# Pool computes the negated score maxima of groups 2 to 31; divisions of the first batch and the mask rows change their places

## The reference

```python
# layer 0, per batch
xn  = x * rsqrt(mean(x*x) + 1e-6) * rms_w
xm  = xn * (1 + scale) + shift            # scale, shift = cond @ w_cond
q, k, v = split(xm @ w_qkv);  q, k = rope(q), rope(k)
x   = softmax(q k^T / 4) v @ w_out + x
# layer 1, per batch
xn  = layer_norm(x)
q, k, v = xn @ q_w + q_b, xn @ k_w + k_b, (xn @ v_w + v_b) * mask
y   = softmax(q k^T + (1 - mask) * -1e6) v
h   = silu(layer_norm(y) * (1 + scale1) + shift1) @ out_w + out_b
out = x + h
```

## Time and profile before

| what | us |
|---|---|
| median of three runs | 509.48 |
| the profiled execution | 507.94 |
| its span, first to last instruction | 506.1 |
| TensorE busy | 486.6 |
| VectorE busy | 397.9 |
| ScalarE busy | 343.6 |
| Pool busy | 301.4 |

### The profile page before, as it was taken

How to read it: one execution, slowest core, us unless ns; L and a number is a source line. 1 busy time by engine, 2 the same in 40 slices (tenths; PEclk the granted TensorE clock), 3 DMA queues, 4 the chain that set the end, 5 groups by cost and what they waited for, 6 DMA issues and landing times.

```text
span 506.1 us, 9691 instructions
## 1 busy us (share of the span) xinstructions
PE 486.6 (96%) x3205; PEld 177.7 (35%) x3205; DVE 397.9 (79%) x1030; ACT 343.6 (68%) x676; POOL 301.4 (60%) x387
## 2 busy tenths in 40 slices
PE   8999899999699999999999999999999999999997
PEld 3554322332153233332342233433333333332234
DVE  3867887988768679875889679986899999999224
ACT  2652467758548677676858677686778778777863
POOL 6479958999977672479507872459882045005401
PEclk9999999999989999999999999999999999999999
DMA  7764255443522443026422352015311112111011
GB/s 250 199 194 174 76 182 177 148 138 119 166 86 65 111 137 100 18 75 178 108 65 66 104 155 70 3 42 149 104 43 45 44 47 83 42 44 44 2 41 41
DMA packets 41577, 49.79 MB, mean 98 GB/s; under 512 B 12388, under 2 KB 34036, under 8 KB 41272
## 3 DMA queue, kind: packets, MB, share of 16 engines
q1 hardware_dynamic: 33336, 31.84, 21.7%
q0 software_dynamic: 7904, 16.03, 10.5%
q10 hardware_dynamic: 288, 1.31, 0.7%
HBM read 27.62 MB, written 19.01 MB: 92 GB/s over the span
## 4 chain that ended last, share of the span: by engine, by line
PE 66%; DVE 20%; DMA 4%; issue 4%; POOL 3%; ACT 2%; SPq 1%; DVEq 0%; POOLq 0%; ACTq 0%
PE bank L602 16%; PE bank L585 11%; PE bank L648 9%; DVE masked L958 9%; PE bank L576 8%; PE bank L564 8%; PE bank L676 5%; DVE row_max L961 5%; PE bank L659 5%; DMA tables<-in_tables 2%; ACT probs L787 1%; PE bank L633 1%; DMA X<-in_x 1%; PE bank L617 1%; DMA k_parts<-parts 1%
## 5 line engine op out<-in xcount | busy, mean ns | idle before, releaser
L787 ACT ACTIVATE probs<-bank 128x512 f32<-128x512 f32 x512 | 271.4, 599 | 82.5 <-PE bank L576 81.4
L961 DVE TENSOR_REDUCE row_max<-bank 128x1 f32<-128x512 f32 x256 | 161.1, 681 | 37.2 <-PE bank L585 37.0
L585 PE MATMUL bank<-k_s,q_s 64*128 64x512 f16 x512 | 182.2, 382 | 4.3 <-DVE row_max L961 2.7
L958 DVE CUSTOM_DVE_ANT_0 masked<-bank,mask_bias 128x512 bf16<-128x512 f32 x256 | 163.1, 687 | 17.6 <-PE bank L585 16.6
L564 PE MATMUL bank<-q_s,k_s 64*128 64x512 f16 x512 | 151.7, 380 | 0.9 <-ACT v_aug L865 0.5
L576 PE MATMUL bank<-shift,kx 64*128 64x512 f16 x512 | 148.5, 376 | 0.9 <-DMA shift<-shift_rows 0.9
L602 PE MATMUL bank<-probs,v_aug 128*17 128x512 f32 x1024 | 135.4, 598 | 0.7 <-ACT probs L787 0.7
L585 PEld LDWEIGHTS bank<-k_s,q_s 64*128 64x128 f16 x512 | 46.2, 93 | 162.6 <-DVE row_max L961 71.7
L648 PE MATMUL bank<-xT,wqkv 128*128 128x512 f32 x128 | 61.7, 612 | 0.8 <-DVE xT L1095 0.6
L576 PEld LDWEIGHTS bank<-shift,kx 64*128 64x128 f16 x512 | 46.7, 95 | 33.2 <-DMA shift<-shift_rows 1.4
L1413 POOL TENSOR_SCALAR scaled<-row_max 128x16 f32<-128x16 f32 x10 | 2.6, 258 | 62.2 <-DVE row_max L958 38.0
(11 more groups left out here) (122 smaller groups left out, 492.5 us busy)
## 6 DMA issues: line engine op xcount, KB each, us to landing
q_s<-q_parts SPq DMA_DIRECT2D x32, 256.0 KB, 3.4
k_s<-k_parts SPq DMA_DIRECT2D x32, 256.0 KB, 4.3
k_parts<-parts POOLq DMA_DIRECT2D x62, 128.0 KB, 3.2
q_parts<-parts POOLq DMA_DIRECT2D x60, 128.0 KB, 3.4
X<-in_x SPq DMA_DIRECT2D x4, 512.0 KB, 8.1
O<-oT SPq DMA_DIRECT2D x64, 32.0 KB, 2.4
roped<-inverses SPq DMA_DIRECT2D x16, 128.0 KB
y<-X SPq DMA_DIRECT2D x7, 256.0 KB, 2.2
```

The source lines that it names most:

```text
L585: nc.tensor.matmul(bank, m.q_s[slot][rows, i, queries], m.k_s[slot][rows, i, :], start=True, stop=True).then_inc(q.d_made, 1)
L787: act.activation(m.probs[k][:, h, :], bank, ACT.Exp, scale=1.0 if s >= B * NG else float(DH) ** -0.5)\
L958: dve.tensor_tensor_reduce(m.masked[D["max", n, k, h] % ND][:, :], bank, m.mask_bias[:, b, :], 1.0, LOWEST, ALU.add, ALU.max, to)\
L961: dve.tensor_reduce(to, bank, AX.X, ALU.max).then_inc(q.d_done, 1)
```

## The change

- `POOL_SHIFTS` begins at 2: Pool does `negate` for groups 2 to 31, and VectorE for 0 and 1 only.
- The rotations are written out one by one, with the `negate`s between them. One given to `rope` stands between its subtraction and its transfers.
- `divide(0, 0)` stands behind rotation (3,0), where it stood behind (3,1); `divide(0, 1)` behind (3,1), where it stood behind (3,2).
- The mask's operations on Pool stand behind `negate(2)`, as they stood behind the wait for it; SP's four mask rows go out in step 7, where they went in step 2.
- In `project(b)` four `negate`s are put in: behind the normalisation, ahead of the first split, ahead of the last split, and (batches 0 to 2) at the end. `negate(22)` moves from the last stage into `project(3)`, ahead of its last split.

```diff
-POOL_SHIFTS = list(range(22, GROUPS))
+POOL_SHIFTS = list(range(2, GROUPS))
...
+    def negate(n):
+        i = POOL_SHIFTS.index(n)
+        pool.wait_ge(q.d_done, maxed(n))
+        pool.wait_ge(q.a_made, A["shift", n - 2] + 1)
+        if i:
+            pool.wait_ge(q.pool_shift, i)
...
-    def rope(b, i):
+    def rope(b, i, *shifts):
...
         pool.tensor_tensor(m.parts[:, 1, i, :], x[:, :], m.parts[:, 0, i, :], ALU.subtract).then_inc(q.part_pool, 1)
+        for n in shifts:
+            negate(n)
         send_parts(b, i)
...
-    for b in range(1, B):
-        for i in range(b == 1, 4):
-            if b == 1 and i >= 2:
-                pool.wait_ge(q.shift_made, i - 1)
-            rope(b, i)
-            if b == B - 1 and i in (1, 2):
-                divide(0, i - 1)
-        if b == 1:
-            pool.wait_ge(q.shift_made, 3)
-            pool.wait_ge(q.mask_in, 32)
...
+    for i in range(1, 4):
+        if i >= 2:
+            pool.wait_ge(q.shift_made, i - 1)
+        rope(1, i)
+    negate(2)
+    pool.wait_ge(q.mask_in, 32)
...
+    rope(2, 0, 3)
+    rope(2, 1, 4)
+    rope(2, 2, 5)
+    rope(2, 3)
+    negate(6)
+    rope(3, 0)
+    divide(0, 0)
+    negate(7)
+    rope(3, 1)
+    divide(0, 1)
+    rope(3, 2)
+    rope(3, 3)
...
     def project(b):
+        s = 6 + NG * b
         rstd("p1", b)
         normal("p1", b)
+        negate(s + 2)
         if b < LAST:
             divide(b + 1, 0)
...
         if b:
             add_bias(b - 1, 1)
-        for i in range(4):
+        negate(s + 3)
+        for i in range(3):
             split(B + b, i)
+        negate(s + 4)
+        split(B + b, 3)
         add_bias(b, 0)
         if b < LAST:
             divide(b + 1, 1)
+            negate(s + 5)
...
     for b in range(LAST):
-        negate(NG * (B + b) + 6)
         if b == 0:
             add_bias(LAST, 1)
+        else:
+            negate(NG * (B + b) + 6)
...
-        if s == 2:
+        if s == 7:
             sp.wait_ge(q.mask_step, 4)
```

More of the change, by code:

```diff
@@ L1229, in rstd @@
         pool.wait_ge(q.rstd_step, 2 * done + 2)
+    def negate(n):
[4 more added lines that the diff above has]
+            pool.wait_ge(q.pool_shift, i)
+        high, low = m.neg_max[n % 2][:, :, 0, :, :], m.neg_max[n % 2][:, :, 1, :, :]
+        pool.tensor_scalar(m.scaled[:, :, :, :], m.row_max[n % 2][:, :, :, :], -1.0 / UNIT, None, ALU.mult)\
+            .then_inc(q.pool_high, 1)
+        pool.wait_ge(q.pool_high, 2 * i + 1)
+        pool.tensor_copy(high, m.scaled[:, :, :, :]).then_inc(q.pool_high, 1)
+        pool.wait_ge(q.pool_high, 2 * i + 2)
+        pool.tensor_tensor(low, m.scaled[:, :, :, :], high, ALU.subtract).then_inc(q.pool_shift, 1)
     def send_parts(pu, i):
@@ L1346, in gpsimd @@
     pool.tensor_tensor(m.es[:, :, :], m.es[:, :, :], m.condT[:, :, :], ALU.mult).then_inc(q.es_step, 1)
-    for b in range(1, B):
-        for i in range(b == 1, 4):
-            if b == 1 and i >= 2:
-                pool.wait_ge(q.shift_made, i - 1)
-            rope(b, i)
-            if b == B - 1 and i in (1, 2):
-                divide(0, i - 1)
-        if b == 1:
-            pool.wait_ge(q.shift_made, 3)
-            pool.wait_ge(q.mask_in, 32)
[L1359 to L1367, removed]
+    for i in range(1, 4):
[4 more added lines that the diff above has]
+    pool.wait_ge(q.mask_in, 32)
+    pool.tensor_scalar(m.mask_bias[:, :, :], m.mask_bias[:, :, :], -1.0, MASK_VALUE, ALU.add, ALU.mult)\
+        .then_inc(q.mask_step, 1)
+    pool.tensor_scalar(m.mask_row[:, :], m.mask_row[:, :], -1.0, MASK_VALUE / UNIT, ALU.add, ALU.mult)\
+        .then_inc(q.mask_step, 1)
+    pool.wait_ge(q.mask_step, 2)
+    pool.tensor_copy(m.mask_part[0][:, :], m.mask_row[:, :]).then_inc(q.mask_step, 1)
+    pool.wait_ge(q.mask_step, 3)
+    pool.tensor_tensor(m.mask_part[1][:, :], m.mask_row[:, :], m.mask_part[0][:, :], ALU.subtract)\
+        .then_inc(q.mask_step, 1)
+    rope(2, 0, 3)
[10 more added lines that the diff above has]
+    rope(3, 3)
     def modulation():
```

## The result

| | before | after |
|---|---|---|
| median of four runs | 509.53 us | 523.73 us (522.69 to 525.5) |
| ratio | | 1.0287, 95% interval 1.0255 to 1.032 |
| the profiled execution | 507.94 | 525.5 |
| its span | 506.1 | 523.6 |

The change makes the kernel 2.9% slower. The forecast was 522.1, range 517.5 to 526.5. The profiled execution is the slowest of the four.

The account below looks back on a forecast made before the run. Pool's ordered queue bounds TensorE at y(0,0); elsewhere TensorE and VectorE run level. Terms 6.5 − 1.5 + 6.0 + 1.6 = +12.6 us on 507.94 give 520.5, plus 1.54 for the median: 522.1, range 517.5 to 526.5.

Parts of the forecast that it names:

- The first wait: TensorE at y(0,0), first piece of step 6, waiting for Pool's second division: stall about 10 us instead of 4.73.
- M(7) + 9.9 = 141.8: M(7): group 7's maxima complete, about 131.9; negation 0.80, rotation 7.87 and division 1.22 then release TensorE at 141.8.
- Just in time: Pool reaches negation 7 at M(6) + 9.9, while M(7) − M(6) is 10.4 less 0.4.
- The second wait: Step 7, transposition of group 8's maxima (L610): TensorE stands 3 to 4 us for negation 8, ending at 166.8, 6.5 later.
- VectorE's pairs: Pairs of small VectorE operations (L969, L971) moved to Pool; groups 12, 16, 20 gain about 0.5 each, 1.5 together.
- The 3.0 gained ahead of step 6: Pairs of groups 3, 4, 6 (2.0 us) and the shift-row wait (0.9) bring M(7) forward 3.0, bounds 2.0 and 3.6.
- Batches 1 to 3: Second projections with negations ahead of splits: cost 0; if Pool's spare went, 1 to 2 us a batch.
- The third wait: Step 22, f1 of batch 0 (L633), waiting for Pool's normalisation: 6.0 us later, bounds 5 and 6.5.
- The clock: One fall of TensorE's clock after the third wait, charged 1.6 us, bounds 0 and 3.2.
- The row gives no reason to charge it: No slow clock charged after the second wait, 3 to 4 us, being shorter than the only stall with a fall.
- The rival of a second fall: Clock falls again after step 7's wait, or stays low longer after step 22: 523.7, up to 525.3; chance 0.17.
- The unfavourable ends of the range: Gain 2.0, pairs 0.5, third stall 6.5 and clock 3.2, put at about 527.3.

Follow-up runs that it names:

- negation 7: The changed kernel with negation 7 behind the second division instead of ahead of rotation (3,1): 522.55 us, ratio 1.0269 to the kernel before.
- the mask rows alone: The kernel before with only the mask rows moved from step 2 to step 7: 508.87 us, ratio 0.9984.
- the negations from group 8 on: The kernel before with Pool's negations from group 8 on and `project(b)` as in the changed kernel; opening, divisions, mask rows as before: 515.10 us, ratio 1.0103.
- negation 22 put back: The changed kernel with group 22's negation back behind the first bias addition of project(3): 517.36 us, ratio 1.0148 to the kernel before.
- combined: Third-wait-removed version plus VectorE negating up to group 8, divisions one rotation earlier, modulation behind batch 0's normalisation, mask rows in step 7: 499.26 us, ratio 0.9821.

## Why the prediction was right

*The first wait.* "M(7) + 9.9 = 141.8": the negation began at 132.31 and L676 at 142.32, 10.0 later. The lag of 3.05 was forecast as 2.5. "Just in time" for negation 7 held too: Pool waited 0.70 us for it. The reason given beside it, "the wait is fixed by Pool's own queue", is borne out; that negation 7 makes it was too narrow, as it is worth 1.45 us by its experiment. From the mask's operation to the second division Pool took 63.3 us (77.57 to 140.90) and 60.7 before. One rotation less stands ahead of the division (7.9 us less), but five negations (4.0) and 6.4 us of waits for maxima are added: +2.5, measured 2.6. The remaining 0.4 of the lag is the mask's transfer, which landed that much later in this execution.

*The second wait.* Forecast: L610 of group 8 at 166.8, behind 3 to 4 us. Measured 167.34 and 3.92.

*VectorE's pairs.* Forecast 0.5 each for groups 12, 16, 20, 1.5 together; measured 0.68, 0.72 and 0.41, 1.8. The 3.0 gained ahead of step 6 was 2.6 in the trace: TensorE came to y(0,0) at 131.90 where it came at 134.54. It entered the sum only through M(7), and two experiments (the mask rows alone, negation 7) show how little of such a gain passes a wait for Pool.

*Batches 1 to 3.* Forecast cost 0: the lag falls by VectorE's pairs alone between groups 9 and 20.

*The third wait.* Forecast 6.0, measured 6.23; negation 22 ahead of the last split makes the greater part of it, shown by moving it alone. The rest (1.87 us of wait) fits negation 21, but that one was moved only together with a bias addition, so its share is not shown.

*The clock.* This is the term that was mis-sized. I charged one fall of 1.6; it was 2.76 behind the third wait and 1.54 behind the second. "The row gives no reason to charge it" was the failed step: from one stall of 4.73 us with a fall I took that a shorter one has none. The rival of a second fall (chance 0.17) came true, with its price of 523.7, and the low stretch was longer too. The Trainium skill's page TensorE: Matmul & The Clock Gate, section "What's actually happening", has the slow clock as the default which activity must release; in this kernel the trace agrees at each of the three waits (0.50 behind each).

*The sum, and luck.* The forecast of 522.1 lies 1.6 below the median, but the sum of +12.6 is 3.0 short of the 15.56 by which the last addition came later in the two traces. The clock is 2.7 of this, the second wait 0.5, the third 0.2, and VectorE's pairs and the last stretch take 0.5 off. What made up for half of it is the 1.54 us that I added because the profiled execution of before was that much below its median. The changed kernel shows no such offset: its profiled execution, without the 1.9 us behind the last addition, would have taken 523.6, and its median is 523.73. So the three waits were read rightly, and part of the closeness is luck. The unfavourable ends of the range, moreover, add up to 526.2 and not to 527.3 (1.0, 1.0, 0.5 and 1.6 above 522.1).

## What to carry to other kernels

A share of 60% says nothing on whether an engine has room where the work is to go: read its timeline in that stage, and mark which of its results another engine waits for last. On an engine that works a list in order, a small operation costs what it waits for, and everything behind it pays; put it behind whatever is due sooner, even if the operation itself takes 0.8 us. Only where the engine would stand still for something else at that place anyway, as for the mask's transfer at negation 2, is the wait free. And a gain ahead of a stall counts only if the engine that ends the stall gets earlier too.

## What was not expected of the hardware

A TensorE wait of 1.87 us was followed by a stretch at a clock of 0.56, and one of 3.92 us by 3.3 us at 0.50, where I had expected the short ones to go free. The wait of 6.68 us was followed by 6.1 us of it, longer than the 3.5 us behind the 4.73 us stall of before.

The length of the wait alone doesn't set the price. Behind the third wait of the changed kernel (6.68 us) the low clock lasted until 392.4, 6.1 us after L633, and cost 2.8 us. Behind the same wait with the negations from group 8 on (6.71 us) it lasted 4.5 us after L633 and cost 2.1. The first row is of the changed kernel, ahead of L633; the second of the other, behind it:

```profile
382.20:386.30 4.10, 0.00 (x0) 0.03 (x1) 0.00 (x0) 0.00 (x0) 4.02 (x5) 0.50 0.00 0
```

```profile
378.00:382.50 4.50, 4.49 (x20) 1.26 (x22) 2.11 (x5) 1.71 (x4) 2.35 (x5) 0.50 0.00 0
```

In both the clock had fallen while TensorE still stood, where it costs nothing: in the changed kernel from 382.2 on, 4.1 us ahead of the start. Behind the wait of 1.87 us (negation 22 put back) it was low for 3.4 us and cost 1.5. In these three the price goes with how much of the low stretch is left when TensorE starts again (3.4, 4.5 and 6.1 us).

The first operation of a negation on VectorE (L969) took between 0.17 and 1.18 us in the kernel before. The trace shows with what the long ones go together: the five that start while Pool is inside a `TENSOR_TENSOR` (groups 0, 4, 5, 6, 7) all end 0.03 us after it, group 4's at 99.86 behind a rotation's operation that ends at 99.83, while every one that starts with no Pool operation running takes 0.17. In combined group 4's starts during a cast and takes 0.18. No run here varied this alone, so the cause is not shown.
